# Asking for x one step ahead instead of two, and storing two steps later from a third buffer

## The reference

```python
Tb = T[fwd_steps - 1]
return jnp.einsum('bij,bjk->bik', Tb, x)
...
x = x + _L0_cond_ref(x, itok_B_1_98, L0_cond_T)
```

## Time and profile before

| | |
|---|---|
| Time, median of 3 runs | 103.3 us (103.22 to 103.64) |
| Profiled execution, its own time | 102.88 us |
| Span of the instructions in it | 101.1 us |
| PE busy | 95.7 us (95% of the span) |
| DVE busy | 87.0 us (86%) |
| POOL busy | 73.1 us (72%) |
| ACT busy | 65.4 us (65%) |
| Moved by DMA | 25.30 MB, mean 250 GB/s |

### The profile page before, as it was taken

One profiled execution on the slowest core, in us unless ns is written; L12 is line 12 of the kernel. 1 busy time (PEld: TensorE's weight loads), 2 busy tenths in 40 slices (PEclk: granted clock), 3 DMA queues, 4 the chain that ended last, 5 costly groups with the idle time before them and its releaser, 6 DMA issues.

```text
span 101.1 us, 1833 instructions
## 1 busy us (share of the span) xinstructions
PE 95.7 (95%) x440; PEld 79.2 (78%) x440; DVE 87.0 (86%) x101; ACT 65.4 (65%) x87; POOL 73.1 (72%) x38
## 2 busy tenths in 40 slices
PE   3999999999999999999999999999999999999950
PEld 3996888888888888887887888888888888888840
DVE  0168889999999999989999999999999999993250
ACT  0957598858585969677676767696867768462100
POOL 2004199999979797978989898989797989908100
PEclk9999999999999999999999999999999999999998
DMA  2899798889999879999999999999999782505074
GB/s 58 288 309 389 191 276 221 257 237 333 302 305 282 264 173 341 252 274 325 246 348 285 319 221 351 217 313 288 284 321 283 250 302 67 211 0 207 6 286 129
DMA packets 22125, 25.30 MB, mean 250 GB/s; under 512 B 2402, under 2 KB 16994, under 8 KB 22114
## 3 DMA queue, kind: packets, MB, share of 16 engines
q10 hardware_dynamic: 4850, 15.34, 47.6%
q1 hardware_dynamic: 17264, 9.84, 36.6%
HBM read 16.78 MB, written 8.39 MB: 249 GB/s over the span
## 4 chain that ended last, share of the span: by engine, by line
PE 87%; DMA 5%; SPq 3%; issue 0%; DVE 0%
PE same L470 29%; PE same L459 28%; PE diff L481 28%; DMA T_sb<-T 5%; SPq L170 2%; PE turned L444 2%; SPq L155 1%; PE diff L491 1%; PE same L491 0%; DVE out_sb L415 0%
## 5 line engine op out<-in xcount | busy, mean ns | idle before, releaser
L302 POOL TENSOR_TENSOR xL<-x_sb,xH 128x1024 fp32r<-128x1024 f32 x14 | 33.8, 2416 | 6.2 <-ACT xH L211 6.1
L318 POOL TENSOR_TENSOR TD_r<-TH_r,TL 128x1024 fp32r<-128x1024 f32 x14 | 33.9, 2420 | 4.1 <-issue 3.7
L470 PE MATMUL same<-xL,TL 128*128 128x512 f32 x128 | 34.6, 392 | 0.0
L459 PE MATMUL same<-xH,TH_r 128*128 128x512 f32 x128 | 34.4, 391 | 0.0
L481 PE MATMUL diff<-xD,TD_r 128*128 128x512 f32 x124 | 33.2, 390 | 0.0
L247 ACT ACTIVATE diff<-same 128x512 f32<-128x512 f32 x31 | 18.1, 583 | 22.4 <-PE same L470 15.8
L358 DVE STREAM_TRANSPOSE turned<-T_sb 128x512 f32<-128x512 f32 x28 | 29.7, 1110 | 0.6 <-DMA T_sb<-T 0.4
L459 PEld LDWEIGHTS same<-xH,TH_r 128*128 128x128 f32 x128 | 23.9, 188 | 5.4 <-ACT TH_r L225 0.3
L470 PEld LDWEIGHTS same<-xL,TL 128*128 128x128 f32 x128 | 23.7, 188 | 5.2 <-DVE TL L380 0.3
L481 PEld LDWEIGHTS diff<-xD,TD_r 128*128 128x128 f32 x124 | 23.3, 188 | 4.9
L388 DVE TENSOR_TENSOR out_sb<-x_sb,diff 128x512 f32<-128x512 f32 x31 | 21.5, 693 | 3.9 <-PE diff L481 3.9
(11 more groups left out here) (29 smaller groups left out, 21.0 us busy)
## 6 DMA issues: line engine op xcount, KB each, us to landing
out<-out_sb ACTq DMA_DIRECT2D x15, 512.0 KB, 6.3
T_sb<-T SPq DMA_DIRECT2D x112, 64.0 KB, 4.9
x_sb<-x ACTq DMA_DIRECT2D x13, 512.0 KB, 5.9
x_sb<-x SPq DMA_DIRECT2D x2, 512.0 KB, 6.0
x_sb<-x ACTq DMA_DIRECT2D x2, 256.0 KB, 2.8
T_sb<-T SPq DMA_DIRECT2D x2, 256.0 KB, 4.7
T_sb<-T SPq DMA_DIRECT2D x1, 512.0 KB, 6.3
out<-out_sb SPq DMA_DIRECT2D x1, 256.0 KB, 2.6
```

The lines of the kernel that those rows point to most:

```text
L302: nc.gpsimd.tensor_tensor(half(xL, h), x_sb[b % X_SLOTS][:, i:i + 2], half(xH, h).bitcast(fp32), ALU.subtract).then_inc(xL_ready, 2)
L318: nc.gpsimd.tensor_tensor(TD_r[s][:], TH_r[s][:].bitcast(fp32), TL[s][:].bitcast(fp32), ALU.subtract).then_inc(TD_ready, 2)
L459: nc.tensor.matmul(same[U % 2][:], TH_r[p][:, i, j], xH[s][:, j], start=(j == 0), stop=False)
L470: done = nc.tensor.matmul(same[U % 2][:], TL[p][:, i, j], xL[s][:, j], start=False, stop=(j == N - 1))
```

## The change

Four things change:

1. In step k ACT asks for half k + 3 instead of half k + 4. Half 4 is still asked for ahead of the loop, so step 1 asks for nothing, and half 15 is asked for in step 12 instead of 11. The wait ahead of the load is rewritten to fit.
2. In step k ACT stores half k - 3 instead of half k - 1. Steps 13 and 14 store two halves each (10 and 11, 12 and 13), so that the output of entry 7 is alone behind the loop, as before.
3. out_sb has three slots instead of two.
4. TH_r, TL and TD_r have three sets instead of four.

```diff
-    X_SLOTS, T_SLOTS, X_SETS, T_SETS, OUT_SLOTS = 4, 3, 3, 4, 2
+    X_SLOTS, T_SLOTS, X_SETS, T_SETS, OUT_SLOTS = 4, 3, 3, 3, 3
...
+        def stored_halves(k):
+
+            return {13: [10, 11], 14: [12, 13], 15: []}.get(k, [k - 3] if k >= 3 else [])
...
-                if k + 4 < 2 * B:
-                    if b >= 2:
-                        act.wait_ge(sum_ready, (b - 1) * N)
-                    load_x_half(act, k + 4)
+                if 5 <= k + 3 < 2 * B:
+                    if k + 3 >= 2 * X_SLOTS:
+                        act.wait_ge(sum_ready, ((k + 3) // 2 - X_SLOTS + 1) * N)
+                    load_x_half(act, k + 3)
                 seed(2 * k + 1)
                 for h in copied_halves(k):
                     copy_xH_half(h)
-                if k < PAIRS - 1:
-
-                    act.wait_ge(sum_ready, 2 * k)
-                    store(act, (k - 1) // 2, slice(2, N) if k % 2 == 0 else slice(0, 2), stored[(k - 1) // 2 % OUT_SLOTS])
+                for h in stored_halves(k):
+                    act.wait_ge(sum_ready, 2 * h + 2)
+                    store(act, h // 2, slice(2, N) if h % 2 else slice(0, 2), stored[h // 2 % OUT_SLOTS])
```

More of the change, by code:

```diff
@@ L269, in _ @@
             for k in range(1, PAIRS):
-                b = k // 2
                 seed(2 * k)
```

## The result

The changed kernel takes 109.2 us (median of 6 runs, 108.66 to 110.62) against 103.3 us before (102.99 to 103.64). The ratio is 1.057, with a 95% interval of 1.0525 to 1.0614: 5.7% slower. The profiled execution took 108.66 us, with a span of 106.9 us instead of 101.1. The predicted 105.3 had the sign and the mechanism, but the time lies above the range (102.9 to 108.0), and the loss of 5.9 us is three times the predicted 1.95.

The account below looks back on a forecast made before the run. PE's back-to-back matmul groups, fed by DVE without slack, were taken as the bound. Late x +2.5, leeway -0.25 and T in time -0.3 make +1.95 on 102.88, so 104.8, or 105.3 as median; range 102.9 to 108.0.

Parts of the forecast that it names:

- What bounds the kernel: In the loop, PE's groups run back to back, 0.907 us apart; DVE has no slack, and TL waits behind TH_r and xH.
- The leeway of 0.25 us: Time from TL's end to PE's weight load that needs it, taken off the loss once.
- Buffers and the stores of steps 13 and 14 cost nothing: Three T sets, the third out_sb slot and the doubled stores near the end: 0 us.
- T in time wins 0.3 us: Fewer bytes queued early put T ahead, ending a transpose's 0.39 us wait at 43.95 us: gain 0.3, between 0 and 0.34.
- The path of a late x: TL to TL two steps on takes at least L + 6.05; second form, a step is L + 0.1, larger from L = 5.85.
- L: Time from issue to landing of an x load: expected between 5.0 and 6.1 us, taken as 5.5; break-even 4.8.
- the term of late x: x asked for one step later: seven loads, of steps 4 to 10, meet T and cost 0.35 us each, 2.5 us.
- (L - 4.8) / 2: Added length of each loop step when x lands later than the break-even of 4.8 us: 0.35 us by L = 5.5.
- The signs: Expected in the profile after: xH waits for x, TL for TH_r, steps of 5.6 to 6.0 us, last T before 76.
- B: Rival: x is hidden anyway, landing in 4.3 us, so only T's gain is left: 103.0 us, chance 0.25.
- C: Rival: it is faster, as T ahead of time wins 0.76 us: 102.5 us, chance 0.08.
- D: Rival: x later than today's, L at 6.1 or more in steps 2 to 10: 109.8 us, chance 0.12.

Follow-up runs that it names:

- run 2: The changed kernel with its x loads as before (half k + 4 in step k), so only stores and buffers change: 103.4 us, ratio 0.9982.
- run 1: The kernel before with the late x loads alone, its stores, two output slots and four T sets kept: 110.4 us, ratio 1.0615.
- run 5: The changed kernel with the x load issued ahead of the two cuts, right behind seed(2k): 103.5 us, ratio 0.9992.
- runs 7 to 9: The changed kernel without the stores of halves 0 to 13 (104.9 us), without the T loads of entries 3 to 7 (103.0), without both (102.7).
- Runs 10 to 12: Store of steps 3 to 12 moved: behind the x load in the changed kernel (113.0 us) or run 5 (107.0), ahead of xH in the changed kernel (110.6).
- run 6: The changed kernel with the x load issued behind seed(2k+1) instead of ahead of it: 115.2 us, ratio 1.1095.

## Why the prediction was too low

- **What bounds the kernel**, PE and DVE side by side with TL behind TH_r behind xH: right. DVE's waits for TH_r, 5.7 us, account for the 5.8 us of span. (TL is line 382 of the changed file, not the 384 of the prediction.) The leeway of 0.25 us that the sum took off does not show: TL came 5.8 us later in all, and the span grew by as much.
- **Buffers and the stores of steps 13 and 14 cost nothing**: right within the 0.2 us that run 2 leaves for a loss.
- **T in time wins 0.3 us**: not shown. Run 2 measures 0.9982 with 1 inside its interval. In the changed kernel no transpose waits for T, but whether that won anything can't be told apart from late x.
- **The path of a late x**: right in its first form. L + 6.05 from TL to TL two steps on gives 41.57 for step 5 (30.02 + 5.5 + 6.05, the load being that of 34.0 us) where 41.62 was measured, and 53.67 for step 7 (41.62 + 6.0 + 6.05, the load of 45.6 us) where it was 53.79.
- **The failed step is the term of late x, +2.5 us, which measured 6.1.** It was mis-sized in four ways. First, "the load itself is issued about 0.1 behind xH, and a step is L + 0.1": it is 0.21 from xH to the issue and about 0.07 from landing to xH, so a step is L + 0.28. That bound overtakes the other from L = 5.5, not 5.85, and a step then costs L - 5.16 and not (L - 4.8) / 2: at 5.9 us it is 0.74 instead of 0.55. Second, L: I took 5.5, and the median was 5.8, with 6.3 and 6.5 in the last two loads that met T. Longer steps did not make it shorter there. Third, the number of steps: SP was to send its last T load before 76 us and sent it at 78.0, so an eighth load, at 76.45 us, met T and stores and was the slowest of all. Fourth, (L - 4.8) / 2 spreads a late x over two steps, which holds only if L is the same in each. Steps 5 to 7 lost 0.7, 0.0 and 1.3 us, the whole L - 4.8 of the loads with 5.5 and 6.0, because DVE doesn't win back in step 6, whose load took 5.1, what step 5 cost.
- **What each was worth.** By the prediction's own rules, the seven loads with the L that they had give 3.5 us instead of 2.5, and the eighth makes it 4.6. Of the other 1.5, some 0.8 is the halving in steps 5 to 7 (2.0 measured, 1.2 by the rules) and 0.7 the step of L + 0.28 in steps 8 to 12 (4.2 measured, 3.5 by the rules). The largest piece is therefore L, with the eighth load: 2.1 of the 3.6 us.
- Step by step from TL to TL the loss over 5.44 us is 0.7, 0.0, 1.3, 0.5, 0.7, 0.3, 1.2, 1.4 and 0.0 us in steps 5 to 13, 6.1 in all. With the loss as L - 5.16, the five loads for steps 8 to 12 (5.7, 5.9, 5.5, 6.3 and 6.5) give 0.54 + 0.74 + 0.34 + 1.14 + 1.34 = 4.1 us, where the trace has 4.2.
- **The signs.** xH waited for x in step 1 and in steps 5 to 12, not in 3 or 4 to 11; the longer steps, 5 and 7 to 12, were 5.8 to 6.8 us from TL to TL, not 5.6 to 6.0; x loads took 5.1 to 6.5 us, not 5 to 6.
- **Rivals.** B (hidden anyway) is out: beside T and nothing else, without stores, an x load took 4.8 us and not 4.3. C (faster) is out, at 1.057. The figure lies next to D's 109.8, though not by D's words: L was under 6.1 in most steps, and the issue behind xH did the rest.
- **Sure and open.** That the loads one step ahead make the loss is shown by runs 1, 2 and 5, and that T and stores together make them late by runs 7 to 9. Why a store adds 0.1 us to L without T and 1.0 with it is not settled: the DMA engines' share of 1.05 speaks for a lack of room, but it is that of the kernel before. In the changed kernel it is 0.92 and L is hardly shorter, 5.8 against 5.9, so the share alone doesn't explain it. Runs 10 to 12 don't settle it, as a store was in flight at each load in all of them.

No version that does the whole work beats the kernel before: run 5 equals it, at 0.9992.

## What to carry to other kernels

If a load is issued behind the instruction that waits for the previous load, its lead isn't counted in steps but closes a loop: a step can't be shorter than the landing time plus what lies between wait and issue (here L + 0.28). Issue the load ahead of that wait; moving one DMA ahead of the two cuts gave the 5.7% back. Look also at what the DMA is held by in its engine's order: it goes out with the last wait ahead of it, not with the last instruction (run 6). Before a load is moved later, take its landing times from the loaded stretch, upper end included, and not from the quiet start; here, at a share of 0.92, a load took half as long again as alone (5.8 against 3.7 us). And where a late load's cost can't be caught up, sum it load by load: a mean hides it.

## What the runs showed of the hardware

- An x load of 512 KB with nothing beside it took 3.7 us, while a lone store of the same size took 2.8. I had priced the one by the other. The trace doesn't say why.
- The Trainium skill, "DMA: Bandwidth & Descriptors", section "Issuing engines are not separate DMA queues", says that transfers issued from different engines run on the same 16 DMA engines and interleave. The runs agree: T, on SP's queue, lengthens x, on ACT's, from 3.7 to 4.8 us.
- ACT sends a DMA before the compute instructions ahead of it in its order have started: 0.8 us ahead of TH_r in the changed kernel (57.88 and 58.64), and in run 6 at the start of TH_r (64.14 and 64.10), 0.9 us ahead of the seed(2k+1) that stands between them. It doesn't pass a wait that isn't met: 0.21 us behind xH's wait for x in the changed kernel, 0.11 to 0.14 us behind the sum_up that the seed waits for in the eleven loads of run 6 from 25 us on.
